# A gated state-space layer on one core: next weights' transposes behind the scan, the first low part behind the second y, output banks in another order

## What is computed

```
proj = einsum('bld,pd->blp', hidden_states, in_proj_w)
gate, hbc, dt = proj[..., :I], proj[..., I:I + CONV_DIM], proj[..., -H:]
conv = conv_bias + sum_k pad(hbc)[:, k:k + L, :] * conv_weight[:, k]
xBC = silu(conv)                                  # x, B, C
dt_p = softplus(dt + dt_bias); dA = exp(dt_p * -exp(A_log))
state = state * dA_t + (dt_p * x)_t * B_t;  y_t = state @ C_t
y = y + x * D
yn = y * rsqrt(mean(y * y, by group) + EPS) * norm_weight * silu(gate)
out = einsum('bli,di->bld', yn, out_proj_w)
```

## Time and profile before

| what | value |
|---|---|
| median of 3 runs | 3395.06 us |
| lowest, highest | 3393.29, 3395.44 us |
| the profiled execution, its own time | 3393.82 us |
| its span in the trace | 3392.1 us |
| mean granted clock of TensorE | 0.998 of full speed |
| busy: PE, PEld, DVE, ACT, POOL | 98%, 81%, 81%, 49%, 13% of the span |

### The profile page before, as it was taken

One profiled execution on the slowest core, in us unless ns is written; L12 is line 12 of the kernel. 1 busy time (PEld: TensorE's weight loads), 2 busy tenths in 40 slices (PEclk: granted clock), 3 DMA queues, 4 the chain that ended last, 5 costly groups with the idle time before them and its releaser, 6 DMA issues. The chain is left out here.

```text
span 3392.1 us, 85994 instructions
## 1 busy us (share of the span) xinstructions
PE 3308.2 (98%) x33306; PEld 2739.2 (81%) x33306; DVE 2753.9 (81%) x4687; ACT 1653.4 (49%) x2947; POOL 444.9 (13%) x328
## 2 busy tenths in 40 slices
PE   8999999999999999999999999999999999999999
PEld 6788888888888888888888888888888877788888
DVE  6888888888888888888888888888888878887443
ACT  5666664555444554445544455444554544544111
POOL 1111111011111011110111101111011110111333
PEclk9999999999999999999999999999999999999999
DMA  7433263234433353335433363235332442225331
GB/s 272 171 120 122 104 231 130 111 136 167 155 135 115 127 201 120 136 117 186 144 115 136 117 210 126 109 136 204 124 136 104 172 147 86 95 78 155 94 93 59
DMA packets 207792, 466.28 MB, mean 137 GB/s; under 512 B 35134, under 2 KB 80606, under 8 KB 198284
## 3 DMA queue, kind: packets, MB, share of 16 engines
q1 hardware_dynamic: 206364, 464.72, 39.0%
q0 software_dynamic: 368, 0.85, 0.1%
q10 hardware_dynamic: 1024, 0.27, 0.0%
HBM read 313.68 MB, written 152.09 MB: 137 GB/s over the span
## 5 line engine op out<-in xcount | busy, mean ns | idle before, releaser
L1123 PE MATMUL low_banks<-ht,wt 128*128 128x512 f32 x6912 | 1612.9, 391 | 0.8 <-DVE xc L1357 0.8
L1123 PEld LDWEIGHTS low_banks<-ht,wt 128*128 128x128 f32 x6912 | 1292.5, 188 | 274.9 <-DVE xc L1357 1.5
L1357 DVE SCALAR_TENSOR_TENSOR xc<-low_banks,cvw,xc 128x496 f32<-128x496 f32 (+2 forms) x1152 | 813.3, 715 | 27.3 <-ACT xc L1255 0.2
L1211 PE MATMUL bank<-wot,gy 128*128 128x512 f32 x3072 | 733.9, 394 | 52.6 <-DVE gy L1406 52.6
L1211 PEld LDWEIGHTS bank<-wot,gy 128*128 128x128 f32 x3072 | 567.1, 188 | 193.4 <-DVE gy L1406 79.2
L1255 ACT ACTIVATE xc<-low_banks,cvb,cvw 128x512 f32<-128x512 f32 x384 | 299.3, 780 | 530.9 <-PE low_banks L1123 530.9
L1075 POOL TENSOR_TENSOR r<-rv,neg_half 128x4 f32<-128x4 f32 x64 | 88.7, 1386 | 2320.8 <-DVE rv L1442 2320.8
L1234 ACT ACTIVATE xc<-xc 128x512 f32<-128x512 f32 x384 | 236.0, 630 | 153.4 <-DVE xc L1357 148.6
L1069 POOL TENSOR_TENSOR segr<-adts,mask_le 128x1024 fp32r<-128x1024 f32 x128 | 242.8, 1917 | 425.6 <-DVE adts L1340 425.6
L1245 ACT ACTIVATE gy<-z 128x512 fp32r<-128x512 f32 x256 | 161.8, 632 | 267.6 <-DVE z L1423 267.6
L1418 DVE TENSOR_TENSOR y<-xc,low_banks 128x512 f32<-128x512 f32 x256 | 174.5, 682 | 94.6 <-PE low_banks L1140 94.6
(11 more groups left out here) (194 smaller groups left out, 3315.0 us busy)
## 6 DMA issues: line engine op xcount, KB each, us to landing
ht<-h_d SPq DMA_DIRECT2D x63, 2048.0 KB, 8.0
acc_d<-acc SPq DMA_DIRECT2D x64, 1024.0 KB, 4.3
wt_d<-wnext SPq DMA_DIRECT2D x112, 512.0 KB, 3.1
acc<-acc_d SPq DMA_DIRECT2D x56, 1024.0 KB, 7.0
wt<-wt_d SPq DMA_DIRECT2D x70, 512.0 KB, 8.7
stage<-in_L_attn_in_proj_w SPq DMA_DIRECT2D x84, 256.0 KB, 2.7
wot<-wt_d SPq DMA_DIRECT2D x28, 512.0 KB, 6.4
xb<-in_x SPq DMA_DIRECT2D x8, 1024.0 KB, 7.6
```

What stands on the lines that cost most here:

```text
L1123: ins = pe.matmul(pb[:, :], wt[:, n, l, k, :], ht[:, rr, k, :], start=(q == 0 and k == 0), stop=(q == 2 and k == KC - 1))
L1211: ins = pe.matmul(bank[OUT[t]][:, :], gy[:, c, l, t * P:(t + 1) * P], wot[:, rr, c, :], start=(c == 0 and q == 0), stop=(c == CT - 1 and q ...
L1357: ins = dve.scalar_tensor_tensor(dst, src, cvw[:, n, TAPS - 1 - k:TAPS - k], dst, ALU.mult, ALU.add)
```

## The change

Four edits. On TensorE the eight transposes of the next weights move from ahead of the scan to behind it, ahead of `project(9)`, and the one wait for both low halves of the next weights, which stood ahead of all output products, becomes a wait for each of the two banks ahead of the first product into it. The output banks `OUT` go from (5, 6, 7, 4) to (7, 5, 6, 4). On ScalarE the high halves of the next weights move behind the four skips, one on each side of `high(0)`, and the square is written apart from the high half. On VectorE the low halves of the next weights move from ahead of the first y to behind `low(0)` and behind the second z; `low(0)` moves from behind the second z to right behind the second y, and the others likewise; the wait for `s_dnp` moves ahead of the wait for the scan; the sums of squares are spread, and `pair(6)` and `pair(7)` stand behind all of them. The queue's list isn't changed.

```diff
@@ -895,7 +895,7 @@
     sh.acc_at = TOP + WT_BYTES + HT_BYTES
 
     bank = sh.bank
-    XT, SEG, CB, OUT, SSQ, NEXT = (4, 5, 6, 7), (4, 5), 3, (5, 6, 7, 4), 3, (5, 6)
+    XT, SEG, CB, OUT, SSQ, NEXT = (4, 5, 6, 7), (4, 5), 3, (7, 5, 6, 4), 3, (5, 6)
     scanned = sh.low_banks
 
 
@@ -1180,22 +1180,21 @@
             pe.wait_ge(s_conv, NCV * it + NCV)
             project(NCV + CT - 2)
 
-            for u in range(2 if prepare else 0):
-                pe.wait_ge(s_raw[u], 16 * it + 16)
-                pe.wait_ge(s_dtx, TT * it + 2 + u)
-                for k in range(KC):
-                    ins = pe.transpose(bank[NEXT[u]][:, k * P:(k + 1) * P], stage[u][:, k * P:(k + 1) * P], sh.ident[:, :])
-                ins.then_inc(s_nps, 1)
             pe.wait_ge(s_cbm, it + 1)
             pe.wait_ge(s_dtx, TT * it + TT)
             pe.wait_ge(s_z, CT * it + CT + 3)
             for c in range(CT):
                 ins = scan(c)
             ins.then_inc(s_yp, 1)
+            for u in range(2 if prepare else 0):
+                pe.wait_ge(s_raw[u], 16 * it + 16)
+                for k in range(KC):
+                    ins = pe.transpose(bank[NEXT[u]][:, k * P:(k + 1) * P], stage[u][:, k * P:(k + 1) * P], sh.ident[:, :])
+                ins.then_inc(s_nps, 1)
             project(NCV + CT - 1)
 
-            if prepare:
-                pe.wait_ge(s_nlo, 2 * it + 2)
             for c in range(CT):
                 if c == CT - 1:
                     pe.wait_ge(s_y, CT * it + 2 * CT)
@@ -1207,6 +1206,8 @@
                 for t in range(TT):
                     if c == 0 and OUT[t] == PROJ_BANK[NCV + CT - 1]:
                         pe.wait_ge(s_z, CT * it + 2 * CT)
+                    elif c == 0 and prepare and OUT[t] in NEXT:
+                        pe.wait_ge(s_nlo, 2 * it + NEXT.index(OUT[t]) + 1)
                     for q, (l, rr) in enumerate(PASSES):
                         ins = pe.matmul(bank[OUT[t]][:, :], gy[:, c, l, t * P:(t + 1) * P], wot[:, rr, c, :],
                                         start=(c == 0 and q == 0), stop=(c == CT - 1 and q == 2))
@@ -1243,8 +1244,16 @@
             def high(c):
                 act.wait_ge(s_u, CT * it + c + 1)
                 act.activation(gy[:, c, 0, :], z[:, c, :], ACT.Copy).then_inc(s_uhi, 1)
+            def square(c):
                 act.activation(y[:, c, :], y[:, c, :], ACT.Square).then_inc(s_sq, 1)
 
+            def next_high(u):
+                if prepare:
+                    act.wait_ge(s_nps, 2 * it + u + 1)
+                    act.wait_ge(s_nst, 32 * it + 32)
+                    act.activation(wnext[:, u, 0, :], bank[NEXT[u]][:, :], ACT.Copy).then_inc(s_nhi, 1)
 
             act.activation(warm[:, :], sh.ones[:, 0:1], ACT.Silu)
             for n in range(NCV):
@@ -1270,17 +1279,19 @@
             skip(1)
             gate(2)
 
-            for u in range(2 if prepare else 0):
-                act.wait_ge(s_nps, 2 * it + u + 1)
-                act.wait_ge(s_nst, 32 * it + 32)
-                act.activation(wnext[:, u, 0, :], bank[NEXT[u]][:, :], ACT.Copy).then_inc(s_nhi, 1)
             skip(2)
             skip(3)
+            next_high(0)
             high(0)
+            next_high(1)
+            square(0)
             high(1)
+            square(1)
             gate(3)
             high(2)
+            square(2)
             high(3)
+            square(3)
             act.wait_ge(s_sqturn, it + 1)
             act.wait_ge(s_rv, it + 1)
             for t in range(TT):
@@ -1396,10 +1407,13 @@
             join(2, la, lc)
             join(1, lb, ld, 9)
 
-            for u in range(2 if prepare else 0):
-                dve.wait_ge(s_nhi, 2 * it + u + 1)
-                dve.tensor_tensor(wnext[:, u, 1, :], bank[NEXT[u]][:, :], wnext[:, u, 0, :].bitcast(F32),
-                                  ALU.subtract).then_inc(s_nlo, 1)
+            def next_low(u):
+                if prepare:
+                    dve.wait_ge(s_nhi, 2 * it + u + 1)
+                    dve.tensor_tensor(wnext[:, u, 1, :], bank[NEXT[u]][:, :], wnext[:, u, 0, :].bitcast(F32),
+                                      ALU.subtract).then_inc(s_nlo, 1)
             def low(c):
 
                 dve.wait_ge(s_uhi, CT * it + c + 1)
@@ -1409,20 +1423,19 @@
 
                 return plane.rearrange("p (t b l) -> p b t l", t=TT, l=L)
 
-            for c in range(CT):
-                if c == 0:
-                    dve.wait_ge(s_yp, it + 1)
-                    dve.wait_ge(s_dnp, 16 * NDP * g + 16 * NDP)
+            def add_skip(c):
+                dve.wait_ge(s_yp, it + 1)
                 dve.wait_ge(s_skip, CT * it + c + 1)
                 dve.tensor_tensor(by_residue(y[:, c, :]), by_residue(xc[:, 2 + c, :]),
                                   scanned[:, :, c * P:(c + 1) * P].rearrange("p b (t l) -> p b t l", l=L),
                                   ALU.add).then_inc(s_y, 1)
+            def gated(c):
                 dve.wait_ge(s_z, CT * it + CT + c + 1)
                 dve.wait_ge(s_y, CT * it + CT + c + 1)
                 dve.scalar_tensor_tensor(z[:, c, :], z[:, c, :], nw[:, c:c + 1], y[:, c, :], ALU.mult, ALU.mult).then_inc(s_u, 1)
-                if c > 0:
-                    low(c - 1)
 
             def add_squares(c):
 
@@ -1431,12 +1444,26 @@
                     dve.wait_ge(s_sqsum, (CT - 1) * it + c - 1)
                 dve.tensor_tensor(y[:, 0, :], y[:, 0, :], y[:, c, :], ALU.add).then_inc(s_sqsum, 1)
 
+            dve.wait_ge(s_dnp, 16 * NDP * g + 16 * NDP)
+            add_skip(0)
+            gated(0)
+            add_skip(1)
+            low(0)
+            next_low(0)
+            gated(1)
+            next_low(1)
+            add_skip(2)
+            low(1)
+            gated(2)
             add_squares(1)
-            low(CT - 1)
+            add_skip(3)
+            low(2)
+            gated(3)
+            add_squares(2)
+            low(3)
+            add_squares(3)
             pair(6, lc, 10)
-            add_squares(2)
             pair(7, ld, 11)
-            add_squares(3)
             dve.wait_ge(s_ssq, it + 1)
             w8_step(13)
             dve.tensor_scalar(rv[:, :], ssum[:, :], 1.0 / GI, EPS, ALU.mult, ALU.add).then_inc(s_rv, 1)
```

## The result

The changed kernel takes 3427.5 us (median of 4 runs, 3426.1 to 3430.9), the kernel before 3395.2 (4 runs beside them, 3393.3 to 3395.4): a ratio of 1.0098, interval 1.0080 to 1.0115. The ratio is the one on record for the runs; the two medians alone give 1.0095. The change makes the kernel slower by 1.0%, as forecast (3426 us). The profiled execution has a span of 3425.1 us, 33.0 over the one before, at a granted clock of 0.997.

The account below looks back on a forecast made before the run. TensorE, busy 98% of the span, was taken as the bound, so only its waits count. Output products 0, queue 19 and first group 12 sum to +31 us on 3393.8, 3425, stated as 3426 us; range 3394 to 3442.

Parts of the forecast that it names:

- Transposes and scan: TensorE: the scan gains 0.12 us; transposes behind it cost about 1.0, so output could load at 3.66 after the mark.
- VectorE and ScalarE: Output products: low(0) done at 3.10, gate(3) at 6.07; last tile loads at 6.02 instead of 5.92; sum +0.3 us.
- The old wait: TensorE's wait for low(0) ahead of the output products, 79.2 us in 63 cases, goes; waits only change names.
- The last eight passes: Passes without next_low: last output tile loads at 5.42 instead of 5.75, a gain of 0.33 us each.
- The queue: SyncE: ht issued at 6.18 instead of 3.09, behind the stores, lands at 15.8; 0.4 us a pass, 19 us in 48.
- Rival B: ht starts its slow part under the stores, lands between 14.2 and 14.8; 3395 to 3400 us, no change; chance 0.26.
- the slow beginning: Start of the ht load at 218 GB/s, taken as its own first packets' and not hidden by the stores; 1.6 us late.
- Rival C: Rival B holds and gate(3) is done before 5.6, so no wait in bank 4; gain 20 us, 3375; chance 0.09.
- D: ht lands nearer 9.0 than 8.0 us behind issue besides the 1.6; about 1.0 more a pass, 3480 us; chance 0.08.
- The first group: Eight passes where x loads behind ht: project(3) 1.2 us late, with ht's 0.4 they lose 1.5 each, together 12 us.

Follow-up runs that it names:

- experiment 2: Changed kernel with the load of ht ahead of the low-half wait and both stores, and gate(3) ahead of high(1): 3385.2 us, ratio 0.9973.
- experiment 3: Changed kernel with only gate(3) moved ahead of high(1), queue's list as in the changed kernel: 3428.9 us, ratio 1.0096.
- Experiment 1: Changed kernel with the load of ht ahead of the wait for both low halves and the two stores of wnext: 3407.4 us, ratio 1.0039.
- experiment 5: Changed kernel with a third store of 512 KB ahead of the two stores in the queue: 3498.1 us, ratio 1.0304.
- experiment 4: Changed kernel with the load of ht still behind the low halves and a 16-byte-a-partition store, but ahead of the two big stores: 3443.3 us, ratio 1.0146.
- experiment 6: Changed kernel with one store of wnext ahead of the load of ht and the other behind it: 3430.3 us, ratio 1.0109.
- the best one: Kernel before plus the new order of low, moved waits, spread sums, gate(3) ahead of high(1), banks (7, 5, 4, 6); transposes and queue unchanged: 3351.9 us, 0.9875.

## Why the prediction was right

*Transposes and scan.* Scan: right, it starts 0.12 earlier against `project(8)`. The transposes were cheaper than said, 0.86 and not 1.0, so the output could load at 3.52 instead of 3.66. It didn't matter: the third tile then waits 0.19 for the second low half, where I had put a few hundredths at most, and the last one waits for the gate anyway.

*VectorE and ScalarE.* `low(0)` done at 3.14 (3.10), the second low half at 5.00 (4.98), `gate(3)` at 6.08 (6.07), the last tile's loads at 6.13 (6.12). The old wait did only change its name; experiment 2 prices it, 0.4 us a pass, and experiment 3 shows that it was hidden under the wait for `ht`. The last eight passes gained 3.5 us (2.6).

*The queue.* The step that decides held: stores at 5.17 (5.14), `ht` issued at 6.18 (6.18), landed at 15.71 on average (15.8), TensorE right behind it. Counted from its issue, the first of its 128 packets of 16 KB begins at 2.62 (before: 0.96), and the last one ends at 9.18 (7.62), as means over the 48 passes: its data starts 1.66 later, where I had put 1.6, and takes 6.6 us as before. Experiment 1 takes the stores away from ahead of it and with them 22.0 of the 24.2 us of the 48 passes; experiment 5 adds half a megabyte ahead of it and the landing follows by 1.2 us. The term was a little small: the 48 passes lost 24.2 where mine were 19 + 3 = 22, and the time itself had two parts that I had not told apart. The mean landing hides a scatter (14.96 to 17.05 after, 10.7 to 11.8 before), so that a pass starts late by 0 to 1.9; and since a wait can't be negative, an early landing doesn't make up for a late one.

*Rival B* falls, but my reason against it was only half right. I had said that the slow beginning belongs to the load's own first packets and so would stay whole behind the stores. It didn't: the first 16 packets take 0.86 us each instead of 1.30, and the second window of the pass moved 369 GB/s, where the earlier trace rows have 218. The later packets took back what that gave; in the pass shown, one of the late ones, the last window moved only 25 GB/s, for 2 us. That the load's 6.6 us came out the same is partly luck. (The packet times are read from the DMA records of the traces.) The Trainium skill ("DMA: Bandwidth & Descriptors", on two DMAs through the same engine) says that descriptors in one queue start in order but are pipelined. The trace agrees with the words, since the load's first packets run beside the stores' last ones, but not with the gain that B takes from them: together they landed at mark + 15.7, and not 14.3. The Trainium skill gives the fit of 2.0 us plus bytes at 436 GB/s, from which the estimate of 14.3 comes, for transfers that GpSimd issues (the same page, "Anatomy of one DMA — SWDGE (gpsimd) path"); these are SyncE's. *Rival C* falls with `gate(3)` at 6.08; had it been done by 5.6 nothing would have been won, as experiment 3 shows, since C also needs B. *D* falls as the mean, though single passes (10.8 from issue to landing) are its case.

*The first group.* Predicted 12 us, measured 10.5. Of it 2.4 are waits for `ht`, in two passes only (1.0 and 1.4), where I had 0.4 in each of eight. 6.9 is the wait at `project(3)`, in seven passes, 1.0 each where I said 1.1; the next group's first pass had no such wait. And 1.3 come from the clock again: in pass 0 of after it is at its lower level for 3.4 us, in before it isn't, and the transposes and `project(9)` took 1.57 and 3.17 us there instead of 0.86 and 2.62.

```profile
144.00:147.20 3.20, 3.20 (x49) 2.94 (x41) 2.31 (x4) 1.45 (x3) 0.00 (x0) 0.50 0.02 5
```

One pass with the wait at `project(3)` in the timeline, the conv's chain behind ScalarE's sorting:

```profile
304.66 4.19 ACT L1304 ACTIVATE acc<-z 128x512 f32<-128x512 f32 x4 [1.58 <-DMA z<-in_x]
...
310.27 1.43 ACT L1264 ACTIVATE xc<-low_banks,cvb,cvw 128x512 f32<-128x512 f32 x2
311.07 4.99 DVE L1368 SCALAR_TENSOR_TENSOR xc<-low_banks,cvw,xc 128x496 f32<-128x496 f32 x7 [0.60 <-ACT xc L1264]
...
313.35 2.82 PEld L1123 LDWEIGHTS low_banks<-ht,wt 128*128 128x128 f32 x13 [0.98 <-DVE xc L1368]
```

*Not foreseen.* The first mark comes 1.8 us later, and by 0.4 to 2.7 in every variant, the best one among them. It is the clock in a stage that the change doesn't touch, as shown above. So the close hit of the total, 1.5 us off, is in part luck: 1.8 and 1.3 us of clock, and 2 us more than forecast in the 48 passes, stand against a first group that waited less and last passes that gained more than I said.

## What to carry to other kernels

Moving a small operation later can cost nothing on its own engine and much in a queue served in order: ask of each semaphore which DMA issues stand behind its wait, and count their bytes ahead of the next load that an engine wants. Where two waits end close to each other, removing one shows nothing (experiment 3: 0 us) until the other is gone (experiment 2: 22 us), so judge an edit after the wait that hides it. And when a queue's list is reordered, follow what comes last in it in every phase of the program: in four of twelve runs (experiments 1, 2, 4 and 6) the 48 ordinary passes came out near the forecast and the miss was in the eight that load `x` too.

## What the runs showed of the hardware

- The instruction that issues a load takes longer when stores stand ahead of it unfinished: 0.33 us (median) with none or with them long issued, 0.35 behind half a MB (experiment 6), 0.65 behind 1 MB, 1.10 behind 1.5 MB. Experiment 5's row of line 982:

```profile
L982 SPq DMA_DIRECT2D ht<-h_d x63: 332/1102/1194, 151.1 to 3161.4; - x63
```

- Two transfers in one queue slow each other both ways. The 2 MB of `ht` take 8.0 us alone, 9.1 with 1 MB issued just behind it (experiments 1 and 4), 9.2 to 9.5 behind it. So a store placed behind a load isn't free for that load: some 1.1 us. The two experiments lose it at different places: with the stores issued at once behind the load (4) its first 16 packets take 2.27 us each instead of 1.30 and the rest 0.61 as before; with them issued over 1 us later (1) the first take 1.31 and the later ones 0.77. Why, no run shows.
- Waits of 2.0 to 3.2 us on TensorE at `project(3)` (experiment 4) each came with 3.4 or 6.8 us at the lower of its two clock levels, 1.2 instead of 2.4 GHz; the waits of up to 1.5 us in the changed kernel's passes 1 to 62 came with none. It isn't every wait of that length: experiment 5 has one of 2.4 us without a fall. So a wait can cost more than its length.
- TensorE loads 0.21 us after the landing of a transfer that it waits for (1588.43 to 1588.64); I had put 0.05.
